# Regional attention block on one core: stages set apart by rows, a prologue in its own order, products in quarters

## The reference

```python
n   = group_norm(x)                               # 32 groups of 8 channels, over the whole image
qkv = einsum('nchw,oc->nohw', n, qkv_w) + qkv_b   # q, k, v
a_r = mean of q per region @ mean of k per region # 7 x 7 regions of 8 x 8 cells
idx = top_k(a_r, 4)                               # 4 regions for each of the 49
out = softmax(q * C**-0.5 @ k[idx].T) @ v[idx]    # 8 heads of 32, 64 queries, 256 keys
out = out + depthwise_conv3x3(v) + lepe_b
y   = x + einsum('nchw,oc->nohw', out, out_w) + out_b
```

## Time and profile before

| | |
|---|---|
| three runs, median | 1858.81 us (1853.92 to 1859.41) |
| profiled execution, its own time | 1856.89 us |
| its span in the trace | 1854.9 us |
| granted TensorE clock, mean | 0.985 |
| TensorE busy | 1722.5 us, 93% |
| VectorE busy | 1541.6 us, 83% |
| ScalarE busy | 1529.1 us, 82% |
| POOL busy | 814.2 us, 44% |

### The profile page before, as it was taken

How to read it: one execution, slowest core, us unless ns; L and a number is a source line. 1 busy time by engine, 2 the same in 40 slices (tenths; PEclk the granted TensorE clock), 3 DMA queues, 4 the chain that set the end, 5 groups by cost and what they waited for, 6 DMA issues and landing times.

```text
span 1854.9 us, 72422 instructions
## 1 busy us (share of the span) xinstructions
PE 1722.5 (93%) x24776; PEld 1054.1 (57%) x24776; DVE 1541.6 (83%) x3427; ACT 1529.1 (82%) x4905; POOL 814.2 (44%) x2256
## 2 busy tenths in 40 slices
PE   4969999999999999999999999999999999977776
PEld 2535665666666666566666666656665666644444
DVE  5878898889998999899898999979987888876554
ACT  1538999899988999889988999889998899977775
POOL 1024444444454444444444444544444444444432
PEclk9989999999999999999999999999999999999999
DMA  3223434343434343344443444343433333332332
GB/s 123 82 59 97 133 120 127 104 133 118 133 115 120 117 133 121 112 127 125 123 125 108 131 122 126 116 119 123 125 121 92 116 105 111 107 104 87 107 99 92
DMA packets 157002, 211.43 MB, mean 114 GB/s; under 512 B 17889, under 2 KB 144737, under 8 KB 156641
## 3 DMA queue, kind: packets, MB, share of 16 engines
q1 hardware_dynamic: 141408, 129.71, 24.1%
q0 software_dynamic: 15232, 77.08, 12.7%
HBM read 155.33 MB, written 51.38 MB: 111 GB/s over the span
## 4 chain that ended last, share of the span: by engine, by line
PE 53%; ACT 21%; DVE 16%; issue 5%; DMA 3%; SPq 2%; POOL 0%; POOLq 0%; ACTq 0%; DVEq 0%
ACT probs L435 16%; PE chunk_bank L745 15%; PE s_bank L813 13%; PE pt_bank L826 9%; DVE neg_max L620 8%; PE o_bank L840 6%; PE chunk_bank L756 5%; DVE lepe L524 4%; ACT probs_t L442 4%; PE chunk_bank L771 2%; DMA v_dram<-v_stage 1%; PE o_bank L850 1%; DMA v_sel<-v_dram 1%; SPq L240 1%; DVE stats L541 1%
## 5 line engine op out<-in xcount | busy, mean ns | idle before, releaser
L435 ACT ACTIVATE probs<-s_bank,neg_max 128x256 f32<-128x256 f32 x1568 | 735.5, 479 | 195.0 <-DVE neg_max L620 194.6
L294 POOL COPY k_sel<-k_all 128x128 f32 x1568 | 406.6, 302 | 665.1 <-PE s_bank L813 637.3
L524 DVE SCALAR_TENSOR_TENSOR lepe<-v_band,taps,lepe 128x448 f32<-128x448 f32 x896 | 611.9, 713 | 71.6 <-POOL v_band L320 56.5
L620 DVE TENSOR_REDUCE neg_max<-s_bank 128x2 f32<-128x512 f32 x784 | 506.2, 686 | 96.3 <-PE s_bank L813 93.8
L745 PE MATMUL chunk_bank<-xn,wqkv 128*128 128x448 f32 x1248 | 549.6, 548 | 3.6 <-DVE xn L560 3.6
L826 PE MATMUL pt_bank<-ident,probs 128*128 128x128 f32 x3136 | 492.7, 280 | 15.3 <-ACT probs_t L442 12.8
L442 ACT COPY probs_t<-pt_bank 128x512 f32<-128x512 f32 x784 | 472.0, 602 | 33.3 <-PE pt_bank L826 32.8
L826 PEld LDWEIGHTS pt_bank<-ident,probs 128*128 128x128 f32 x3136 | 361.0, 141 | 188.0 <-issue 112.4
L305 POOL TENSOR_TENSOR lepe<-o_norm,lepe 128x128 f32<-128x128 f32 x392 | 280.9, 717 | 240.4 <-DVE o_norm L638 240.0
L435 ACT ACTIVATION_READ_ACCUMULATOR probs<-s_bank,neg_max 128x1 f32 x1568 | 322.9, 206 | 0.0
L813 PE MATMUL s_bank<-k_sel,q_all 32*64 32x256 f32 x6272 | 270.6, 400 | 23.7 <-ACT probs L435 13.0
(11 more groups left out here) (68 smaller groups left out, 1119.7 us busy)
## 6 DMA issues: line engine op xcount, KB each, us to landing
v_sel<-v_dram SPq DMA_DIRECT2D x1568, 64.0 KB
xn<-x_dram POOLq DMA_DIRECT2D x56, 448.0 KB, 4.6
v_dram<-v_stage SPq DMA_DIRECT2D x112, 224.0 KB
resid<-x_dram POOLq DMA_DIRECT2D x56, 448.0 KB, 4.2
out_dram<-resid POOLq DMA_DIRECT2D x56, 448.0 KB, 3.5
wqkv<-w_qkv_dram SPq DMA_DIRECT2D x1, 768.0 KB, 10.0
wout<-w_out_dram SPq DMA_DIRECT2D x1, 256.0 KB, 11.7
idx_row<-top_idx SPq DMA_DIRECT2D x8, 0.8 KB
```

Of the source, the lines that this page charges most:

```text
L294: last = pool.tensor_copy(k_sel[:, r % K_SLOTS, :, RT * j:RT * (j + 1)], k_all[:, b % 2, :, bass.ds(reg[j] * RT, RT)])
L435: act.activation(probs[:, u, :], s_bank[:, u, 0:KEYS], ACT.Exp, bias=neg_max[:, r % 2, u:u + 1], accum_out=denom[:, r % 2, u:u + 1]).then_ ...
L524: ins = dve.scalar_tensor_tensor(row, v_band[:, n % BANDS, k, t // 3:t // 3 + RS, t % 3:t % 3 + W], taps[:, k, t:t + 1], row, ALU.mult, AL ...
L620: dve.tensor_reduce(neg_max[:, r % 2, 2 * hf:2 * hf + 2], s_bank[:, 2 * hf:2 * hf + 2, 0:KEYS], AX.X, ALU.max, negate=True).then_inc(max_d ...
```

## The change

The leads are set for each stage by itself: v and k seven rows ahead (`KV_LEAD`), q two, outer taps one, middle tap two, `normalize` eight, statistics fourteen. The rings follow: q 2 rows (8 before), convolution 4 (10), v bands 8 (3), x 14 (9), and the staging of turned values is doubled. The middle tap is now a POOL instruction that reads v from SBUF. The prologue is straight code: for image 0 all rows of v with their turns, then q of row 0, then all rows of k, then the first scores. Each chunk is four matmuls of 224 cells (`QUARTERS`), divided among the regions in fives and fours. In the last row of an image the values are turned at regions 3 and 4 (4 and 5 otherwise) and stored at region 5. DVE now takes its taps at the end of each region. The removed lines of the old order are left out below; they stand in the kernel above.

```diff
 K_SLOTS = 2
-RING = NWIN + 1
-X_RING = NWIN + 2
-LEPE_RING = NWIN + 3
-BANDS = 3
+Q_RING = 2
+X_RING = 2 * NWIN
+LEPE_RING = 4
...
+KV_LEAD = NWIN
+Q_LEAD = 2
+TAP_LEAD = 1
+MID_LEAD = 2
+NORM_LEAD = NWIN + 1
+STAT_LEAD = 2 * NWIN
+LOAD_LEAD = 2 * NWIN + 1
+STEPS = ROWS + 1
+QUARTERS = 2 * KC
+HALF = ROW // 2
...
+def early_order():
+    for n in range(NWIN):
+        yield "v", n
+        if n:
+            yield "vt", n - 1
+    yield "vt", LAST
+    yield "q", 0
+    for n in range(NWIN):
+        yield "k", n
+def step_order(s):
+    kv, out, vt, q = s + KV_LEAD, ("out", s - 1), ("vt", s + KV_LEAD), ("q", s + Q_LEAD)
+    if s % NWIN == LAST:
+        return [("v", kv), ("k", kv), vt, out, q]
+    return [("v", kv), ("k", kv), out, vt, q]
...
             def select_values(r):
+                b = r // NREG
+                if r % NREG == 0:
+                    sp.wait_ge(idx_in, 16 * (b + 1))
...
+                if r % NREG == 0:
+                    n = b * NWIN + LAST
+                    sp.wait_ge(v_stored[0], 32 * (n // 2 + 1))
+                    sp.wait_ge(v_stored[1], 32 * ((n + 1) // 2))
...
+            for n in range(NWIN):
+                store_values(n)
+                if n == 3:
+                    load_index(0)
+            select_values(0)
+            select_values(1)
...
+                    if rc == 5 and rr == LAST and is_row(kv):
+                        store_values(kv)
+                    if is_region(r + 2):
                         select_values(r + 2)
-                    if rc == 6 and rr == LAST and is_row(s + A_LEAD):
-                        n = s + A_LEAD
-                        store_values(n)
-                        sp.wait_ge(idx_in, 16 * (n // NWIN + 1))
-                        sp.wait_ge(v_stored, 32 * (n + 1))
-                        select_values(r + 1)
-                        select_values(r + 2)
+                    if rc == 4 and rr == 0 and is_row(kv):
+                        load_index(kv // NWIN)
+                    if rc == 6 and rr != LAST and is_row(kv):
+                        store_values(kv)
...
+            def mid_tap(n, k):
+                wait_taken(pool, "v", n, k)
+                if n >= LEPE_RING and k == 0:
+                    wait_full(pool, "out", n - LEPE_RING, 1)
+                pool.tensor_scalar(in_image(lepe[:, k, n % LEPE_RING, :]),
+                                   v_band[:, n % BANDS, k, 1:1 + RS, 1:1 + W], taps[:, k, MID_TAP:MID_TAP + 1],
+                                   btap[:, k:k + 1], ALU.mult, ALU.add).then_inc(mid_done, 1)
...
+            image_rstd(0)
+            pool.wait_ge(weights_in, 16 * N_WEIGHTS)
+            for n in range(NWIN):
+                halo(n)
+                if n < MID_LEAD:
+                    mid_tap(n, 0)
+                    mid_tap(n, 1)
+            load_x(X_RING)
+            image_rstd(1)
+            gather_keys(0)
+            gather_keys(1)
...
+                    if rc == 0 and is_row(s + LOAD_LEAD):
+                        load_x(s + LOAD_LEAD)
+                    elif rc == 1 and is_row(s + MID_LEAD):
+                        mid_tap(s + MID_LEAD, 0)
+                    elif rc == 2 and is_row(s + MID_LEAD):
+                        mid_tap(s + MID_LEAD, 1)
+                    elif rc == 3:
+                        if rr == LAST and is_row(xr):
+                            image_rstd(xr // NWIN)
+                        if is_row(kv):
+                            halo(kv)
+                    elif rc == 5 and is_row(s):
                         load_resid(s)
-                    if rc == 6 and is_row(s + A_LEAD):
-                        halo(s + A_LEAD)
+                    elif rc == 6 and is_row(s - 1):
+                        store_row(s - 1)
...
                         probs_t_out(r, 0)
                     if rc == 0:
-                        q_out(ar, 1)
+                        if first and s:
+                            q_out(s - 1 + Q_LEAD, 0)
+                        if s:
+                            q_out(s - 1 + Q_LEAD, 1)
                     elif rc == 1:
-                        v_out(ar, 0)
+                        v_out(kv, 0)
+                    elif rc == 2:
+                        v_out(kv, 1)
                     elif rc == 3:
-                        mid_tap(ar, 1)
-                    elif rc == 6:
-                        vt_out(ar, 0)
+                        k_out(kv, 0)
+                    elif rc == 4:
+                        k_out(kv, 1)
+                        if last_row:
+                            vt_out(kv, 0)
+                    elif rc == 5:
+                        vt_out(kv, 1 if last_row else 0)
+                    elif not last_row:
+                        vt_out(kv, 1)
+                        q_out(s + Q_LEAD, 0)
...
+                    dve.wait_ge(mid_done, KC * n + k + 1)
...
+                dve.wait_ge(x_read, 2 * KC * (NWIN * (b + 1) - 1) + KC)
...
+            for n in range(NWIN):
+                row_stats(n)
+            prepare()
+            image_constants(0)
+            for n in range(NWIN):
+                normalize(n, 0)
+                normalize(n, 1)
+            image_sums(0)
+            row_stats(NWIN)
+            row_stats(NWIN + 1)
+            affinity_out(0)
+            choose(0)
+            for i in range(KC * (TAPS - 1)):
+                outer_tap(0, i)
+            for n in range(NWIN + 2, 2 * NWIN):
+                row_stats(n)
+            image_constants(1)
+            normalize(NWIN, 0)
+            normalize(NWIN, 1)
+            image_sums(1)
+            maximum(0, 0)
+            maximum(0, 1)
+            for s in range(STEPS):
...
+                    if rc == 0:
                         x_moments(xr, 0)
+                        outer_tap(now, 0)
+                        outer_tap(now, 1)
+                    elif rc == 1:
+                        x_moments(xr, 1)
+                        outer_tap(now, 2)
+                        outer_tap(now, 3)
+                        outer_tap(now, 4)
                         if ends_x:
                             image_stats(xr // NWIN)
                     elif rc == 2:
+                        x_sums(xr, 0)
+                        outer_tap(now, 5)
                         outer_tap(now, 6)
...
                     elif rc == 3:
+                        x_sums(xr, 1)
+                        outer_tap(now, 7)
+                        outer_tap(now, 8)
+                        if not last_row:
+                            out_half(s - 1, 0)
+                    elif rc == 4:
+                        if last_row:
+                            out_half(s - 1, 0)
+                        normalize(s + NORM_LEAD, 1)
+                        normalize(s + NORM_LEAD, 0)
+                        if not last_row:
+                            out_half(s - 1, 1)
+                    elif rc == 5:
+                        if last_row:
+                            out_half(s - 1, 1)
+                        outer_tap(now, 9)
+                        outer_tap(now, 10)
                         outer_tap(now, 11)
+                    else:
+                        for i in range(12, KC * (TAPS - 1)):
+                            outer_tap(now, i)
...
-            def project(kind, n, k, part):
...
+                for i in range(first, last):
+                    half, part = divmod(i, KC)
+                    cols = slice(HALF * half, HALF * (half + 1))
+                    if i == 0:
+                        pe.wait_ge(row_normed, KC * (n + 1))
+                        wait_bank(pe, kind, n, k)
+                    ins = pe.matmul(bank_of(kind, n, k)[:, cols], wqkv[:, part, col:col + P],
+                                    xn[:, part, n % X_RING, cols], start=(part == 0), stop=(part == KC - 1))
+                if last == QUARTERS:
                     ins.then_inc(full(kind, n, k), 1)
...
+            for n in range(NWIN):
+                project("v", n, 0, 0, QUARTERS)
+                project("v", n, 1, 0, QUARTERS)
+                if n:
+                    turn_v(n - 1, 0)
+                    turn_v(n - 1, 1)
+                if n == 1:
+                    region_means(0)
+                elif n == 2:
+                    affinities(0)
+            turn_v(LAST, 0)
+            turn_v(LAST, 1)
+            project("q", 0, 0, 0, QUARTERS)
+            project("q", 0, 1, 0, QUARTERS)
+            for n in range(NWIN):
+                project("k", n, 0, 0, QUARTERS)
+                project("k", n, 1, 0, QUARTERS)
+                if n == 3:
+                    group_means(1)
+                elif n == 4:
+                    group_vars(1)
+            pe.wait_ge(aff_taken, 1)
+            pe.wait_ge(var_eps, 2)
+            scores(0)
+            project("q", 1, 0, 0, QUARTERS)
+            project("q", 1, 1, 0, QUARTERS)
...
                     if rc == 0:
-                        project("v", ar, 0, 0)
```

(56 more changed lines are left out.)

282 lines of the change are left out of this document (108 added, 174 removed).

## The result

| | before | after |
|---|---|---|
| runs, median | 1858.21 us (4 runs, 1853.92 to 1859.41) | 1802.97 us (4 runs, 1801.49 to 1805.1) |
| ratio to before, 95% interval | | 0.971 (0.969 to 0.973) |
| span of the profiled execution | 1854.9 us | 1803.3 us |
| first scores | 125.78 | 88.20 |
| rows 0 to 48 | 1509.2 | 1496.1 |

The kernel became 55 us faster; the forecast was 1807 (1783 to 1848). In the spans the gain is -37.6 in the prologue, -13.1 in rows 0 to 48, -2.4 in the last rows and +1.5 at the end, -51.6 in all.

A forecast was written before the change was run, and what follows sets the result against it. Rows were bounded partly by TensorE, partly by a 4.0 us loop from scores to scores. 88.7 + 1502.6 + 198.4 + 14.5 = 1804.2 us of span, 2.0 outside, 1806 to 1808: 1807; range 1783 to 1848 (0.8).

The forecast's parts named there:

- Prologue: Up to the first scores: 88.7 us instead of 125.78, with 16 taps and one row of q ahead; -37.1.
- Quarters: Projections: each 448-column product becomes two of 224; 32 more pairs a row cost 0.13 us, loads hidden.
- Evened regions: Ordinary rows: quarters in fives and fours make 29.7 us against 29.85, almost nothing gained.
- the 0.2 added for VectorE: Ordinary rows: allowance for VectorE's new order in regions 1, 3 and 6, between 0 and 1.4; row 29.9 us.
- Image boundaries: First and last rows of images: wait for values goes, 17 us gained, 8 back; extra 46.5 becomes 37.5.
- ScalarE: Each row loses two evacuations of 0.77 us, gaining nothing; 0.1 uncovered where two evacuations precede an exp.
- Middle tap: On POOL twice a row, 1.1 us each, delaying no score; by the skill's rule VectorE would pay 2.2 a row.
- Last seven rows: Taps and q fall here: 6 x 28.4 + 28.0 = 198.4 us against 205.2, -6.8; four taps cost 0.4.
- The end: Behind the last rows: 14.7 us loses at most 0.2, entered in the sum as 14.5.
- The first rival: Windows of regions 1, 3, 6: VectorE bounds a row, 0.5 to 1.4 us more, 1830 to 1873; chance 0.17.
- rivals of exposed loads: Projections: each added weight load exposed, 32 x 0.11 = 3.5 us a row, 1987 in all; chance 0.03.
- a prologue that doesn't shrink: First scores only at 100 to 110 through banks, stores or lower clock; 1820 to 1830 us; chance 0.10.
- The rival of better rows: Ordinary rows of 29.0 to 29.4 us because waits inside the 2.36 go; 1765 to 1785; chance 0.10.

The follow-up runs named there:

- the experiment that puts the time back: Changed kernel with 72 extra VectorE statistics instructions behind the prologue's 16 taps; 1835.22 us, ratio 0.990 to the kernel before.
- the run with whole products: Changed kernel with 448-column products again, four or six quarters' worth a region; 1818.84 us, ratio 0.981 to the kernel before.
- the mended kernel: Changed kernel with one tap out of region 6's window and, in images' last rows, group means before region 1's taps, variances later; 1794.32 us, ratio 0.965.

## Why the prediction was right, point by point

- *Prologue*: right. First scores were forecast at 88.7, seen at 88.20. VectorE's part is shown by the experiment that puts the time back. Two smaller terms were wrong and cancel: TensorE started at 26.45 instead of 27.5, and the first sixteen pairs lost 3.0 us to the lower clock (32.53 - 26.45 against 3.03) instead of 1.7; k ended at 84.0, forecast 83.8.
- *Quarters*: right. Forecast 4 ns for an added pair, seen 0 in a run of pairs (0.189 against half of 0.378) and 0.04 us a row for 32. The Trainium skill ("TensorE: Matmul & The Clock Gate", Part 3: Packing small matmuls, The mechanism) would have exposed each load for want of another row group; these full loads of 128 rows hid behind 224 columns, so the trace still disagrees with it.
- *Evened regions*: right in the arithmetic (29.7 computed, 29.65 seen), but the 0.2 added for VectorE was wrong: in an ordinary row next to nothing is lost (three of 35 take 29.79 to 29.83). The windows of regions 1 and 3 fit, and the one of region 6, which does overrun, is hidden behind the quarters of the next region, as the run with whole products shows. Over the rows the forecast's 29.9 was 49 x 0.24 = 11.8 us too much.
- *Image boundaries*: the wait did go, but the gain was mis-sized, and the cause given is not the only one that would do it. The store does go out earlier, by 4.55 us against attend (15.50 - 10.95, forecast 4.6), and by arithmetic that covers a wait of 1.62. But the words read ahead of the wait take it away by themselves, as the run shows; no run has the early turn without them. It is needed only at the last image and costs 1.4 us at each of the others. I had read the earlier trace rows as a store that is late; reading SyncE's registers behind the wait was enough to cause the delay. In sums, counted above ordinary rows: the first rows of images and row 0 went down by 10.6 us (39.4 to 28.8) where the forecast took 17, and the last rows went up by 6.5 (7.1 to 13.6) where it gave 8 back. With the turn late everywhere the first rows have 6.2 less, so most of what is missing from the 17 is the early turn's own price. Forecast: 37.5 us of extra over 49 ordinary rows; seen: 1496.1 - 49 x 29.66 = 42.8, so 5.3 too few.
- *ScalarE*: right, nothing; and the 0.1 where two evacuations stand before an exp is, by the timeline, the 4.08.
- *Middle tap*: right that it costs a row nothing here. At 0.71 us alone it is cheaper than the 1.1 taken, beside taps dearer (mean of all 1.75), and POOL had room for either.
- *Last seven rows*: rows without a fall of the clock take 28.39, forecast 28.4. What was missing are the falls themselves, 3.2 us in three rows; 0.8 in row 49, where the early turn leaves a region of six quarters (4.84); and 0.4 in the last row, for which the forecast took 28.0 and which has the stall too. Together that is the 4.4 us by which 198.4 fell short of 202.8. The step "q's quarters fit, four taps in one window cost 0.4" priced the stall, but not the clock that falls after it; without the stall (27.97 a row, in the mended kernel) it does not fall.
- *The end*: 16.2 against 14.5. TensorE waits 1.00 for POOL's last sum before the closing output products, where before it began them without a wait, but it has less left to do: the last store lands 15.5 us after the start of the last scores, before 15.9. The time is lost behind it. From that landing to the end of the span it is 4.7 us, before 2.9; the trace has only POOL's closing DRAIN instruction there, 7.3 us from its start against 5.4. Why it takes longer was not found out.

Against the forecast the stages came out at -0.5, -6.5, +4.4 and +1.7 us: the time was met to 4 us and the span to 1 partly because these cancel, and that much is luck. The first rival (VectorE as the bound of a row) fell for the ordinary row, and holds for one distance in each of the last seven. The rivals of exposed loads and of a prologue that doesn't shrink fell. The rival of better rows fell too: 29.65 is above its 29.4, and the fixed part is what it was (4.23 to 4.29 less five quarters of 0.378 is 2.34 to 2.40).

## What to carry to other kernels

- Price an added instruction by the window it stands in, not by its engine's busy share: here the same instruction costs 0.04 us a row in one region and 0.49 in another. Look for the consumer's first instruction behind it (the maxima, 0.8 or 1.04 after the scores), and for how much work TensorE has ahead of its next wait for that engine, which may hide the delay.
- When a transfer comes late, look at everything that its issuing engine does between its waits. Register loads that depend on nothing new belong ahead of the wait.
- A stall in a stretch where TensorE is not full costs more than its length if the clock falls behind it, here 0.8 to 1.2 us beside the stall's 0.4; a stretch at the floor is the first place to look for work that could move elsewhere.

## What the runs showed of the hardware that was not expected

**VectorE's taps and POOL's middle tap beside each other, and either may pay.** POOL's middle tap of 448 columns takes 0.71 us alone (two in 1.42, in the prologue); in ordinary rows, beside two or three two-input taps, it takes 1.69 or 2.21.

```profile
L346 POOL TENSOR_SCALAR lepe<-v_band,taps,btap 128x448 f32<-128x448 f32 x112 | 195.9, 1749 | 0.0
...
33.93 1.42 POOL L346 TENSOR_SCALAR lepe<-v_band,taps,btap 128x448 f32<-128x448 f32 x2
...
864.87 1.86 DVE L591 SCALAR_TENSOR_TENSOR lepe<-v_band,taps,lepe 128x448 f32<-128x448 f32 x3
...
864.94 2.21 POOL L346 TENSOR_SCALAR lepe<-v_band,taps,btap 128x448 f32<-128x448 f32 x1
```

In the changed kernel POOL pays in 41 of the 42 cases with three taps. In the mended one, where nothing but the order of VectorE's work differs, there are 36 such cases: POOL pays in 20, and in 16 the third tap takes 0.97 instead of 0.68 and POOL only 1.6. In all of them the first tap starts 0.07 or 0.08 us before POOL's instruction, so that order does not tell the two outcomes apart. In the last rows, where the tap beside it starts 0.38 ahead, while POOL's instruction before is still running, both pay a little: the tap takes 0.88 and POOL 1.08 or 1.53. The Trainium skill ("SBUF — State Buffer", Who interferes with whom) says that VectorE with two SBUF inputs and a reading GpSimd contend; these rows agree. The prediction had worked out from it that VectorE would pay 2.2 us a row, and had not taken that into its sum; VectorE pays nothing, 0.2 or 0.3 at a time (and once, at 768.5 us of the mended kernel, a single tap took 1.62 beside a POOL instruction of 0.71), because mostly it is POOL that waits. What decides between them was not found out.

**Reading chosen words into SyncE's registers** ahead of the wait, in the kernel before, brings the gather 1.9 us nearer to the store (5.82 to 3.94).

**The granted clock after a short stall.** In the last rows the clock fell to 1.2 GHz behind idle pieces of 0.98, 0.34 and 0.27 us within one region, in three rows of seven, for 3.4 to 6.8 us. With the usual pieces of the floor (0.56, 0.34 and 0.27 in each region) it did not fall in any of the mended kernel's last six rows. The kernel before had a case between these: a fall of 3.4 us at 1689.3, behind 0.80, 0.34 and 0.27.
